# A chunked delta-rule scan on one core: values made ahead of the mixing, a wider retrieval, and context loads moved behind the last rows

## The reference

```python
q, k, v, beta_pre = split(normed @ w_qkvb + b_qkvb, 4)      # 16 heads of 16
beta = sigmoid(beta_pre); k = k / max(norm(k), 1e-6)
def step(S, (q_t, k_t, v_t, beta_t)):                       # S is 16 x 16 for each of 8 x 16 heads
    retrieval = S @ k_t
    S = S + outer(beta_t * (v_t - retrieval), k_t)
    return S, S @ q_t
_, out_t = lax.scan(step, 0, tokens)                        # 512 steps
x = x + out_t @ w_out + b_out
```

## Time and profile before

| | us |
|---|---|
| Median of 3 runs | 899.46 |
| The profiled execution's own time | 901.5 |
| Its span in the trace | 899.6 |
| PE (TensorE) busy, matmuls / weight loads | 766.8 / 552.7 |
| VectorE (DVE) busy | 730.6 |
| ScalarE (ACT) busy | 572.0 |
| GpSimd (POOL) busy | 493.1 |
| Chain that ended last | PE 46%, DVE 41%, issue 8%, ACT 4% |

### The profile page before, as it was taken

One profiled execution on the slowest core, in us unless ns is written; L12 is line 12 of the kernel. 1 busy time (PEld: TensorE's weight loads), 2 busy tenths in 40 slices (PEclk: granted clock), 3 DMA queues, 4 the chain that ended last, 5 costly groups with the idle time before them and its releaser, 6 DMA issues.

```text
span 899.6 us, 31249 instructions
## 1 busy us (share of the span) xinstructions
PE 766.8 (85%) x12284; PEld 552.7 (61%) x12291; DVE 730.6 (81%) x2230; ACT 572.0 (64%) x1536; POOL 493.1 (55%) x594
## 2 busy tenths in 40 slices
PE   7799999999999999998989998899999407994485
PEld 7567677767676677776666666666666204442364
DVE  3888798998996889886978876756777786999897
ACT  4577577766774667674657644457776634992294
POOL 5456666856654747463547444557888724950000
PEclk9999799999996999996999999999999857997599
DMA  9900000000000000040000001442200000000023
GB/s 172 174 5 14 8 11 14 10 15 9 15 9 8 13 11 10 14 146 12 15 8 11 13 8 45 139 140 71 71 1 1 0 1 1 1 1 1 1 83 106
DMA packets 28617, 31.25 MB, mean 35 GB/s; under 512 B 5548, under 2 KB 23864, under 8 KB 28472
## 3 DMA queue, kind: packets, MB, share of 16 engines
q1 hardware_dynamic: 28256, 29.12, 12.7%
q10 hardware_dynamic: 216, 0.14, 0.1%
HBM read 20.85 MB, written 4.19 MB: 28 GB/s over the span
## 4 chain that ended last, share of the span: by engine, by line
PE 46%; DVE 41%; issue 8%; ACT 4%; POOL 1%; DVEq 0%; ACTq 0%; POOLq 0%
DVE arena L1345 5%; DVE arena L1353 5%; PE ps L2141 4%; PE ps L2021 4%; PE psG L1971 3%; DVE arena L1331 3%; PE ps L1946 3%; PE psX L2162 3%; DVE arena L1334 3%; PE psY L2162 2%; PE ps L2352 2%; PE psG L2141 2%; DVE arena L1323 2%; DVE arena L1324 2%; DVE arena L1356 2%
## 5 line engine op out<-in xcount | busy, mean ns | idle before, releaser
L540 POOL TENSOR_TENSOR arena<-arena 128x1024 f32<-128x1024 f32 x32 | 75.8, 2369 | 177.2 <-DVE arena L1334 171.7
L551 POOL TENSOR_TENSOR work<-work,half 128x16 f32<-128x16 f32 x32 | 97.1, 3033 | 2.7
L1971 PE MATMUL psG<-arena 128*128 128x512 f32 x128 | 73.5, 703 | 0.0
L755 ACT ACTIVATE arena<-ps 128x512 f32<-128x512 f32 x64 | 34.7, 594 | 58.9 <-PE ps L2012 58.9
L1353 DVE TENSOR_REDUCE arena<-arena 128x64 f32<-128x256 f32 (+1 forms) x96 | 65.9, 687 | 3.3
L2021 PE MATMUL ps<-arena 128*128 128x128 f32 x384 | 52.7, 289 | 2.4 <-ACT arena L755 1.3
L807 ACT ACTIVATE arena<-ps,columns 128x128 f32<-128x128 f32 x64 | 20.0, 363 | 51.2 <-PE ps L2021 51.2
L2021 PE MATMUL ps<-nT,arena 128*128 128x128 f32 x384 | 49.3, 279 | 3.3 <-ACT nT L815 1.2
L2012 PEld LDWEIGHTS ps<-work 32*64 32x64 f32 x1024 | 29.7, 139 | 36.6 <-issue 34.5
L2021 PEld LDWEIGHTS ps<-arena 128*128 128x128 f32 x384 | 48.4, 201 | 5.7 <-ACT arena L755 4.6
L2012 PE MATMUL ps<-work 32*64 32x128 f32 x1024 | 46.6, 294 | 5.3 <-issue 3.8
(11 more groups left out here) (363 smaller groups left out, 2352.7 us busy)
## 6 DMA issues: line engine op xcount, KB each, us to landing
arena<-in_mask_BxSxS_ik SPq DMA_DIRECT2D x8, 1024.0 KB, 6.6
xs<-arena SPq DMA_DIRECT2D x256, 16.0 KB, 2.1
arena<-in_ctx SPq DMA_DIRECT2D x8, 512.0 KB, 4.2
out<-xs SPq DMA_DIRECT2D x32, 128.0 KB, 1.7
arena<-in_x SPq DMA_DIRECT2D x8, 288.0 KB, 17.1
arena<-in_L_ffn_w SPq DMA_DIRECT2D x2, 1024.0 KB, 22.4
arena<-in_x SPq DMA_DIRECT2D x16, 96.0 KB, 5.9
arena<-in_L_attn_w_qkvb SPq DMA_DIRECT2D x2, 512.0 KB, 5.0
```

The lines of the kernel that those rows point to most:

```text
L540: G.tensor_tensor(keys, keys, same_half.rearrange("p (a t) -> p a t", a=1).broadcast_to([P, NH, HALF]), ALU.mult).then_inc(att_masked, 1)
L551: own(G.tensor_tensor(root, length, half, ALU.pow))
L1971: M.matmul(psG[:, f * 512:(f + 1) * 512], block16[:, :], PF[m % 2][:, f * 512:(f + 1) * 512], start=True, stop=True).then_inc(g1_mm, 1)
```

## The change

`values(j + 1)` is taken out of the place between `turn` and `updates_turned` and put at the end of chunk j's round, behind `keys` and ahead of `mixed(j - 1)`. Its two waits are the same, counted for the chunk it now serves.

`retrieval` streams, for each head, the row of zeros before the keys, the keys and queries, and the row of zeros after them: 96 columns (64 for the first and last head) in place of 32. The zeros are added to the places of the neighbouring heads. The weights (`scopy`) and the number of calls stay.

SP loads the contexts of sequences 2 and 3 after the last rows of chunk 31 and without a wait of their own.

```diff
--- before.py
+++ after.py
@@ -466,13 +466,10 @@
                     sp.wait_ge(ret_mm, NCK)
                     for t, vec in ((xg_s, x_gamma), (xb_s, x_beta), (fg_s, f_g), (fb_s, f_b)):
                         sp.dma_start(t[:, :], everywhere(vec)).then_inc(const_in, 16)
-                if j == NCK - 1:
-                    sp.wait_ge(u_done, NCK)
-                    context(2)
                 sp.wait_ge(x_done, j + 1)
                 for b in range(B):
                     sp.dma_start(xs[c * CT:(c + 1) * CT, w * B + b, :], xc[b * CT:(b + 1) * CT, j, :]).then_inc(xs_in[w], 16)
-            sp.wait_ge(o_mm, NCK)
+            context(2)
             context(3)
             for b in range(4, B):
 
@@ -1981,9 +1978,10 @@
                 for h in range(NH):
                     if h % (NH // 2) == 0:
                         pe.wait_ge(state_copied, 2 * m - 1 + h // (NH // 2))
+                    a, b = 1 if h == 0 else 0, 2 if h == NH - 1 else 3
                     for r in range(4):
                         rows = slice(32 * r, 32 * r + 32)
-                        last = M.matmul(into[rows, h], scopy[rows, h, :], streams[rows, h, 1],
+                        last = M.matmul(into[rows, h - 1 + a:h - 1 + b], scopy[rows, h, :], streams[rows, h, a:b],
                                         start=False, stop=True, skip_group_check=True)
                 last.then_inc(ret_mm, 1)
 
@@ -2207,10 +2205,6 @@
                         state(j - 1)
                 if j >= 1 and exists(j + 3):
                     turn(j + 3)
-                if j >= 2 and exists(j):
-                    pe.wait_ge(oT_ready, j - 1)
-                    pe.wait_ge(c_ready, j - 1)
-                    values(j)
                 if exists(j - 1):
                     updates_turned(j - 1)
                 if j >= 1 and exists(j):
@@ -2261,6 +2255,10 @@
                     if j == 0:
                         values(1)
                     keys(m)
+                if j >= 1 and exists(j + 1):
+                    pe.wait_ge(oT_ready, j)
+                    pe.wait_ge(c_ready, j)
+                    values(j + 1)
                 if exists(j - 1):
                     mixed(j - 1, m)
                 if j == NCK - 1:
```

## The result

The kernel after takes 901.33 us by the median of 20 runs (896.97 to 914.03), the kernel before 898.92 in the same comparison (889.23 to 905.24). The ratio is 1.0065 with a 95% interval of 1.0035 to 1.0094: slower, by a little more than half a percent. The forecast was 898 and a small gain; the sign was wrong. The ratios here leave out runs more than 1.5% above the fastest of the same kernel, so for every kernel the median of all runs is given too, as a difference to the median of the kernel before in the same comparison (here +2.4 us).

The account below looks back on a forecast made before the run. VectorE's solve plus 3.7 us of TensorE set the old chunk, TensorE the new. Thirty chunks gain 4.3 us (486.4 against 490.7), net 2.5 with the chunk before; contexts 0.9: 901.5 less 3.4 gives 898.1, range 882 to 912.

Parts of the forecast that it names:

- The bound: Scan chunk after the change: TensorE bounds it at 16.27 us, against 15.80 for the solve-to-solve chain.
- Zeros: Retrieval with 96 columns in place of 32: 2.80 us, 1.58 more, fully on the path.
- far end of 26.8 ns per matmul: Retrieval: dearest cost of 96 columns, on a line to the attention's matmuls, making the retrieval 3.26 us.
- rival B: Retrieval: 96 columns cost 26.8 ns as in attention, 0.46 us more per chunk, 14 us, 912 in all; chance 0.14.
- near end of 2.45: Retrieval: cheapest cost, the fixed part of 2.9 ns disappears in longer streams, 19.8 ns per matmul, 2.45 us.
- Wait for the state copies: Retrieval waiting for ScalarE's copies of the state: 0.18 us of new wait per chunk, ends 0 and 0.25.
- Stalls: TensorE's issue waits inside retrieval and attention: 0.52 us per chunk falls to 0.1, mostly covered by the zeros.
- The clock: The 30 chunks: clock stays at its upper level, so the 49 us at the lower level go.
- Values: Values moved out from between state product and retrieval: alone worth 0.17 us per chunk, nothing where TensorE is late.
- Contexts: End of the scan: context loads behind the last rows end VectorE's 0.93 us wait; worth 0.9 us.
- Rival C: TensorE's issue stalls are not late instructions and stay 0.52 us per chunk: 911, or 914 with clock falls; chance 0.10.
- Rival D: Zeros do not hold the clock up; 49 us at the lower level cost about 20, 918 in all; chance 0.07.

Follow-up runs that it names:

- loads_at_25: The kernel after with the loads of contexts 0 and 1 (3 MB) at chunk 25 of SP in place of 21; 908.97 us in one run.
- zeros_only: The kernel before with only the retrieval's zeros streamed, values and context loads in their old places; 907.14 us, ratio 1.0159.
- shift128: The kernel before with 32 small matmuls (128 instructions) more in TensorE's warm-up; 905.42 us in one run.
- values_only: The kernel before with only the values moved behind the keys, retrieval at 32 columns, contexts as before; 933.74 us, ratio 1.0424.

## Why the prediction was wrong

**The bound** was read rightly. A chunk of the kernel after was put at 16.27 us with TensorE as the bound and measures 16.18 to 16.21; VectorE waits 1.2 us for the retrieval where the earlier trace rows had 0.17.

**Zeros**: forecast 1.58 us more per retrieval, measured 1.45 (2.67 against 1.22). The far end of 26.8 ns per matmul and rival B are out; 2.67 us lies between the 2.80 taken and the near end of 2.45. The rule of the Trainium skill on small matmuls (TensorEngine Tiling (Array Packing), Instruction Overhead) does not hold here: 32, 64 and 96 columns gave 1.22, 1.87 and 2.67 us.

**Wait for the state copies**: forecast 0.18, measured 0.25 in 27 of the 30 chunks and 0.47 in the last three, so at the upper end of what was allowed.

**Stalls**: "I leave 0.1 of 0.52 per chunk." The pauses that are left, 3.4 us, are about that. But 27 ordinary chunks take 16.36 on the mean against the typical 16.20, so 0.16. The step is a little short, 2.4 us over the scan against my 16.27. The last two chunks were put at 15.8 and 15.0 and took 15.94 and 15.95, 1.1 more.

**The clock** is the step that failed: "That the 49 us go is already in the sum". The term of the falls was put at nothing. They went from 51 to 10 us, and the one fall that is left, with the pause ahead of it, makes a chunk of 21.97 in place of 16.3, 5.7 us. The mechanism was right (the zeros hold the clock) and the size was not. Together these three are the 9.2 us by which the chunks (495.6) exceed the forecast (486.4), and this term is the largest: without its 5.7 us the profile's own time would have gone down by 4, not up by 1.7. I took the pauses as one kind, bounded by 2.1 us and covered by the zeros; the one beside the 3 MB of loads has a cause of its own, and `loads_at_25` shows it.

**The rest of the sum.** The profiled time was put at 898.1 and is 903.2, 5.1 more. That is the 9.2, less 3.4 ahead of the first border and less 0.7 behind the scan. The first border came 1.7 sooner (47.37 against 49.04 us) where 1.8 later was forecast: the first chunk began 1.0 sooner, which had no part in the change (in the other profiles it begins at 26.9 to 28.2 us), and lasted 0.6 less, without the 3.4 us at the lower level that it had before. So luck there hid part of the miss.

**The base of the comparison**: I set 898 against a median of 899.46 and called it a gain of 1.5. That was within the noise of the sign from the start: the runs of the kernel before go from 889.23 to 905.24 us, and one fall of the kind that is left costs four times the gain.

**Values**: "Alone the move would be worth 0.17 us in such a chunk, and nothing where TensorE is late already." Alone it cost 36 us. This is the mechanism I missed, though it does not show in the full change: what the values did for the clock was priced at nothing because the timeline shows them only as time on the path, and the new waits of 0.25 for the state copies and 0.36 for VectorE's near products were not set against the 0.17. Together with the zeros the move gains 0.19 to 0.22 us per chunk, where the slack of 0.55 less the new wait of 0.25 would allow 0.30.

**Contexts**: forecast -0.9, measured 1.6 less behind the scan (358.3 against 359.9 us), in the trace of the kernel after and in that of the part alone. The -3.7 by medians of the part alone is not clear of its spread. In `zeros_only`, where the rows come later, the old order costs a pause of 4.75 us in place of 2.09, and a fall.

**Rival C** is mostly out: the pauses are instruction packets, as their move by 128 instructions and their places in the blocks of 256 show, and 2.7 of 15.7 us are left. The Trainium skill (Runtime: NRT & Kernel Launch, Instruction fetch mechanics) has the size of the blocks right and calls the crossing mostly hidden; in the trace of the kernel before 22 of about 82 borders between 49 and 540 us have a pause, 17.2 us in all. **Rival D** is out: with zeros in every retrieval two profiles have no fall at all in the 30 chunks. Its price for the falls, about 20 us for 49 at the lower level, was right (19.9 for 51.2). Whether the zeros hold the clock by being streamed or by filling the pauses was not separated. The move of the values changed the clock and not the issue waits, but it brought other waits into every chunk, so it does not decide this either.

So the loss adds up like this. In the two profiles, 0.64 us more in each chunk without a fall are +19.2, falls that are gone -14.3, the time ahead of the first border -1.7 and behind the scan -1.6: +1.7 us with the rounding, in which the 1.0 by which the first chunk began sooner is not the change's. Over all runs it is much the same: the median granted clock is 0.952, against 0.930 to 0.932 for the kernel before in the later comparisons, some 38 us less at the lower level, worth 15 to 19 us by the estimate above, against 19.2 paid. The change bought back most of the clock, and paid a little more than that was worth.

## What to carry to other kernels

Before moving dense matmuls out of a stretch of many small ones, ask what they were doing for the instruction fetch and the clock: the price of the move alone was 36 us of 897, and nothing on the path showed it. Work added on the path to hold the clock is best tried at several widths: here half the width of zeros gave much the same clock and 11 us less in the scan. And a sum built from full-speed rows leaves the falls of the clock out. Where one fall is worth more than the gain, as here, it needs a term for the falls that are left, and the median of many runs to compare with.

## What the runs showed of the hardware that was not expected

TensorE's instructions come in packets of 256, 16.4 KB each. A block whose border shows a pause took 2.9 to 4.8 us from border to border in the kernel before (a few without a pause took 2.6 to 3.1), while 32 by 32 matmuls in float32 use 256 instructions in 1.22 us. Each pause ended 1.15 to 1.60 us behind the end of a packet. Beside the load of 3 MB (340 to 387 GB/s in `loads_at_25`) the next packet started late, though it took no longer: none began for 13.5 us in `loads_at_25` and for 8.7 us in the kernel before, in both until the load ended. It is not so in every profile; in `shift128` one began 5.7 us into the load. The pauses beside these loads went up to 3.1 us, those elsewhere up to 2.4.

The same kernel's runs on one core spread by 2 to 3% (876.68 to 901.80 with the contexts moved), where the two kernels with both rows of zeros and the values in their old place spread by 0.7 and 0.9% (904.46 to 910.61, 902.89 to 911.40). The falls of the clock were the noise of this measurement: in the 23 runs of the kernel before beside `values_only`, time and time at the lower level go together with a correlation of 0.97.
